# A reordered opening of a fused attention and FFN kernel: context first, K's and V's projections ahead of the queries', signs on ACT, slot 1 in another order

## What is computed

```python
q = layernorm(x) @ Wq    # 32 heads of 128
k, v = ctx @ Wk, ctx @ Wv    # 8 heads of 128, each shared by 4 query heads
q, k = rotary(q, pos), rotary(k, pos)
a = softmax(where(mask == 0, -1e9, q @ k.T / sqrt(128))) @ v
x = x + a @ Wo
h = layernorm(x)
r = softmax(h @ gate_w.T)        # 8 experts
return x + (h * (r @ in_scale)) @ sign(W).T * (r @ out_scale) + bias
```

## Time and profile before

| | |
|---|---|
| median of 3 runs | 1199.98 us (1199.96 to 1200.46) |
| the profiled execution | 1200.44 us |
| its span, first to last instruction | 1197.4 us |
| PE busy | 1162.7 us, 97% |
| DVE, POOL, ACT busy | 810.1, 712.2, 551.7 us |
| mean granted clock of PE | 0.988 of 2.4 GHz |

### The profile page before, as it was taken

One profiled execution on the slowest core, in us unless ns is written; L12 is line 12 of the kernel. 1 busy time (PEld: TensorE's weight loads), 2 busy tenths in 40 slices (PEclk: granted clock), 3 DMA queues, 4 the chain that ended last, 5 costly groups with the idle time before them and its releaser, 6 DMA issues.

```text
span 1197.4 us, 23749 instructions
## 1 busy us (share of the span) xinstructions
PE 1162.7 (97%) x7636; PEld 951.1 (79%) x7636; DVE 810.1 (68%) x1367; ACT 551.7 (46%) x1768; POOL 712.2 (59%) x593
## 2 busy tenths in 40 slices
PE   5799999999999999999999999999999999999996
PEld 4588888888888888887888888888888888888875
DVE  6767677666776666676766677667667666666663
ACT  3445445444453544444544444544454354444432
POOL 5666655555666655765555675655666565676515
PEclk8899999999999999999999999999999999999997
DMA  8234332232422223433322322323332221222200
GB/s 219 86 110 119 96 98 87 80 92 80 120 89 71 79 79 88 128 101 93 98 76 72 95 90 77 105 80 96 88 98 88 62 79 62 87 83 89 66 2 35
DMA packets 136923, 106.02 MB, mean 89 GB/s; under 512 B 12776, under 2 KB 111080, under 8 KB 136864
## 3 DMA queue, kind: packets, MB, share of 16 engines
q1 hardware_dynamic: 131488, 94.78, 27.0%
q10 hardware_dynamic: 4608, 8.39, 2.1%
q0 software_dynamic: 768, 2.10, 0.5%
HBM read 101.05 MB, written 4.19 MB: 88 GB/s over the span
## 4 chain that ended last, share of the span: by engine, by line
PE 87%; DVE 9%; POOL 2%; issue 1%; ACT 1%; DMA 1%; POOLq 0%; DVEq 0%; SPq 0%; ACTq 0%
PE chunk L1037 23%; PE chunk L1038 22%; PE chunk L1039 22%; PE o_ps L1110 4%; DVE swp L793 3%; PE sc_ps L1085 3%; PE tr_ps L1085 2%; PE aux L1026 2%; PE o_ps L1026 2%; DVE qT L795 1%; PE sc_ps L1026 1%; PE tr_ps L1026 1%; PE aux L1187 1%; PE aux L1188 1%; DVE oT_lo L728 1%
## 5 line engine op out<-in xcount | busy, mean ns | idle before, releaser
L404 POOL TENSOR_TENSOR w_lo<-raw,w_hi 128x512 fp32r<-128x512 f32 x192 | 247.2, 1299 | 385.3 <-ACT w_hi L503 385.3
L793 DVE TENSOR_TENSOR swp<-chunk,sinT 64x512 f32<-64x512 f32 x320 | 220.4, 689 | 98.7 <-PE chunk L1039 94.7
L1037 PE MATMUL chunk<-xT_hi,w_hi 128*128 128x512 f32 (+1 forms) x512 | 211.6, 413 | 2.0 <-POOL w_lo L404 1.9
L1038 PE MATMUL chunk<-xT_lo,w_hi 128*128 128x512 f32 (+1 forms) x512 | 201.9, 394 | 0.0
L1039 PE MATMUL chunk<-xT_hi,w_lo 128*128 128x512 f32 (+1 forms) x512 | 201.1, 393 | 0.0
L1037 PE MATMUL chunk<-wo_hi,oT_hi 128*128 128x512 f32 x496 | 196.6, 396 | 0.4 <-issue 0.4
L411 POOL TENSOR_TENSOR qT<-qT,swp 128x512 f32<-128x512 f32 x128 | 165.9, 1296 | 47.1 <-DVE qT L795 44.9
L1039 PE MATMUL chunk<-wo_hi,oT_lo 128*128 128x512 f32 x496 | 193.7, 390 | 0.0
L1038 PE MATMUL chunk<-wo_lo,oT_hi 128*128 128x512 f32 x496 | 193.2, 390 | 0.0
L539 ACT ACTIVATE probs<-scores,neg_max 128x64 f32<-128x64 f32 x512 | 170.4, 335 | 28.2 <-DVE neg_max L750 28.2
L735 DVE TENSOR_TENSOR acc<-chunk,acc 128x512 f32 (+1 forms) x128 | 88.2, 689 | 139.9 <-PE chunk L1039 139.5
(11 more groups left out here) (281 smaller groups left out, 1936.7 us busy)
## 6 DMA issues: line engine op xcount, KB each, us to landing
raw<-in_L_xattn_Wo SPq DMA_DIRECT2D x132, 256.0 KB, 2.6
raw<-in_L_xattn_Wq SPq DMA_DIRECT2D x128, 256.0 KB, 2.7
raw<-in_L_xattn_Wk SPq DMA_DIRECT2D x32, 256.0 KB
raw<-in_L_xattn_Wv SPq DMA_DIRECT2D x32, 256.0 KB
acc<-in_x ACTq DMA_DIRECT2D x16, 256.0 KB, 2.9
c_tile<-in_ctx SPq DMA_DIRECT2D x12, 256.0 KB, 3.1
x_tile<-in_x SPq DMA_DIRECT2D x12, 256.0 KB, 3.4
result<-y ACTq DMA_DIRECT2D x12, 256.0 KB, 2.1
```

The lines of the kernel that those rows point to most:

```text
L404: nc.gpsimd.tensor_tensor(lo, raw[:, n % RING, :], hi.bitcast(F32), ALU.subtract).then_inc(wsplit_lo, 1)
L793: last = nc.vector.tensor_tensor(swp[to, k, :], bank[of, :], sinT[to, here], ALU.mult)
L1037: nc.tensor.matmul(bank, a_hi, b_hi, start=i == 0, stop=False)
L1038: nc.tensor.matmul(bank, a_hi, b_lo, start=False, stop=False)
```

## The change

- Loads: context tiles 0 and 1 come first on SP's queue, 2 and 3 first on ACT's; then Wk, x tiles 0 and 1, Wv and the queries' weights on SP, x tiles 2 and 3 and the positions on ACT's. ffn_weight is loaded before the mask.
- Slot 0 loads six weights in the order K, V, queries (`FIRST_STREAM`), and none of wo. K is projected right behind the context's transposes; V behind x's and the rotary rows' transposes, then the queries.
- POOL computes s_rstd between the second and the third gather. The zeroing of buffers comes later, and the small FFN tables use other buffers (f_tile, fT).
- The signs are made by ACT (`ACT.Sign`), one instruction each.
- Slot 1 has lists of its own on PE, ACT and DVE (`first_attention`): K's projection before the scores, the others at other places; `scales_lo` and the copies of `ffn_constants` come later.
- The weights' ring in later slots is numbered anew (`ring_use`, `split_count`), with the same distance between a load and the split that it waits for.

```diff
-    PLACE = [STREAM.index(c) for c in range(CH)]
-    assert CH % RING == 0 and PROJ % WRING == 0 and BT == 512 and 2 * S == P and KVH == TJ + PAIRS + 2
+    FIRST_STREAM = [0, PROJ - 1, 1, 2, 3, 4]
...
-        in_raw, out_raw, gate_raw, sign_scratch = vT, probs[:, 0, :], c_tile, probs[:, 1, :]
+        in_raw, out_raw, gate_raw = f_tile, fT, c_tile
...
-        C_BANK, X_BANK = [aux, sc_ps, tr_ps, o_ps[0]], [chunk[0], chunk[2], o_ps[1], aux]
-        ROWS_BANK, SGN_BANK, GATE_BANK = [sc_ps, tr_ps], [sc_ps, tr_ps, o_ps[0], aux], o_ps[1]
+        C_BANK, X_BANK = [aux, sc_ps, tr_ps, o_ps[0]], [chunk[2], o_ps[1], sc_ps, aux]
+        ROWS_BANK, SGN_BANK, GATE_BANK = [tr_ps, o_ps[0]], [o_ps[0], sc_ps, tr_ps, aux], o_ps[1]
...
+        def loads_of(s):
+            return FIRST_STREAM if s.first_proj else STREAM if s.proj else [PROJ + h for h in range(HG)]
+        def ring_use(s, n):
+            return (n % RING, n // RING + 1) if s.first_proj else ((n - HG) % RING, 2 * s.U + (n - HG) // RING + 1)
+        def split_count(s, n):
+            return n + 1 if s.first_proj else s.U * CH - HG + n + 1
+        def rank(s, j):
+            return FIRST_STREAM.index(j) if s.first_proj else j
+        def proj_bank(s, j):
+            return chunk[0 if s.first_proj and j == PROJ - 1 else PROJ_BANK[j]]
...
-                for n in range(CH):
-                    if s.first_proj and n == RING:
-                        load_constants()
-                    c, r = STREAM[n], n % RING
+                for n, c in enumerate(loads_of(s)):
+                    r, _ = ring_use(s, n)
                     if c >= PROJ:
                         grp = (s.g + KVH - 1) % KVH if isinstance(s.g, int) else s.g - 1
                     else:
                         grp = s.g
                     if not (s.first_proj and n < RING):
-                        sp.wait_ge(wsplit_lo, s.U * CH + n - RING + 1)
+                        sp.wait_ge(wsplit_lo, split_count(s, n) - RING)
                     if c < PROJ:
                         src = (wk_c[:, :, bass.ts(grp, D)] if c == 0 else
                                wv_c[:, :, bass.ts(grp, D)] if c == PROJ - 1 else
@@ -331,6 +349,11 @@
                         sp.dma_start(raw[:, r, :].rearrange("p (c n) -> p c n", n=P), src).then_inc(raw_in[r], 16)
                     else:
                         sp.dma_start(raw[:, r, :], wo[bass.ts(grp * HG + (c - PROJ), D), :]).then_inc(raw_in[r], 16)
+                    if s.first_proj and n == 0:
+                        for p in range(2):
+                            sp.dma_start(acc[:, p, :], row_of(x_t, p)).then_inc(x_first_in[p], 16)
+                if s.first_proj:
+                    load_constants()
...
             def load_constants():
+                sp.dma_start(fw, ffn_w.rearrange("(c p) n -> p c n", p=P)).then_inc(fw_in, 16)
                 load_mask(0)
-                sp.dma_start(fw, ffn_w.rearrange("(c p) n -> p c n", p=P)).then_inc(fw_in, 16)
                 sp.wait_ge(zeros_ok, 4)
...
-            sp.dma_start(pos_i[:, :], pos.rearrange("(n b) s -> (b s) n", b=2),
-                         allow_slow_non_contiguous=True).then_inc(pos_in, 16)
-            for p in range(PAIRS):
+                        r, _ = ring_use(s, h)
+                        sp.wait_ge(wsplit_lo, split_count(s, h) - RING)
+                        sp.dma_start(raw[:, r, :], wo[bass.ts((KVH - 1) * HG + h, D), :]).then_inc(raw_in[r], 16)
+            for p in range(2):
                 sp.dma_start(c_first[:, p, :], row_of(ctx_t, p)).then_inc(c_first_in[p], 16)
...
-            wait_alone(pool, pos_first_ok, 1)
-            for p in range(PAIRS):
-                gather_rows(rows_first[:, p, :], pos_first[:, p:p + 1]).then_inc(rows_first_in, 16)
-            for zeros in (gate_raw[:, :], in_raw[:, :], out_raw, route[:, :]):
-                nc.gpsimd.memset(zeros, 0.0).then_inc(zeros_ok, 1)
-            pool.wait_ge(consts, 1)
-            pool.wait_ge(x_st3, PAIRS)
-            nc.gpsimd.tensor_tensor(s_rstd[:, :], s_var[:, :], half[:, :], ALU.pow).then_inc(x_st4, PAIRS)
...
+            def first_projections(s):
+                for n in range(3, PROJ):
+                    split_lo(s, n)
+                    rope_sum(s, n - 3)
+                rope_sum(s, KQ - 2)
+                rope_sum(s, KQ - 1)
             def slot(s):
                 t, f, residual = jobs_of(s)
+                if s.first_proj:
+                    return first_projections(s)
...
+            def first_quarter():
+                first = Slot(0, 0, False, False)
+                split_lo(first, 0)
+                wait_alone(pool, pos_first_ok, 1)
+                for p in range(PAIRS):
+                    if p == 2:
+                        pool.wait_ge(consts, 1)
+                        pool.wait_ge(x_st3, PAIRS)
+                        nc.gpsimd.tensor_tensor(s_rstd[:, :], s_var[:, :], half[:, :], ALU.pow).then_inc(x_st4, PAIRS)
+                    gather_rows(rows_first[:, p, :], pos_first[:, p:p + 1]).then_inc(rows_first_in, 16)
+                split_lo(first, 1)
+                split_lo(first, 2)
+                pool.wait_ge(x_tr, PAIRS)
+                for zeros in (gate_raw[:, :], in_raw[:, :], out_raw[:, :], route[:, :]):
+                    nc.gpsimd.memset(zeros, 0.0).then_inc(zeros_ok, 1)
+                wait_alone(pool, rows_tr, PAIRS)
+                nc.gpsimd.memset(scores[:, :, :], MASKED).then_inc(fill_ok, 1)
+            first_quarter()
...
-                act.wait_ge(proj_done, (s.U + 1) * PROJ)
-                if s.first_proj:
-                    act.wait_ge(sc_lo, 2)
-                else:
+                act.wait_ge(proj_done, s.U * PROJ + rank(s, PROJ - 1) + 1)
+                if not s.first_proj:
                     act.wait_ge(v_tr, s.U)
-                copy(vT[:, :], chunk[PROJ_BANK[PROJ - 1]][:, :]).then_inc(vT_ok, 1)
+                copy(vT[:, :], proj_bank(s, PROJ - 1)[:, :]).then_inc(vT_ok, 1)
...
+            def first_attention(s):
+                ffn_constants()
+                split_hi(s, 0)
+                split_hi(s, 1)
+                v_in_rows(s)
+                split_hi(s, 2)
+                exp_duo(s, 0)
+                exp_duo(s, 1)
+                for n in range(3, 6):
+                    split_hi(s, n)
+                pT_hi_split(s, 0)
+                split_hi(s, 6)
+                split_hi(s, 7)
+                pT_hi_split(s, 1)
+                out_hi(s, 0)
+                out_hi(s, 1)
+                split_hi(s, 8)
+                split_hi(s, 9)
+                v_out(s)
+                out_hi(s, 2)
+                out_hi(s, 3)
+            def first_projections(s):
+                split_hi(s, 3)
+                v_out(s)
+                split_hi(s, 4)
+                act.wait_ge(fw_in, 16)
+                for c in range(EC):
+                    nc.scalar.activation(fw[:, c, :], fw[:, c, :], ACT.Sign).then_inc(fw_sgn, 1)
+                split_hi(s, 5)
...
-                act.wait_ge(sc_in, 16 * 6)
-                copy(in_sc[:, :], in_raw[:, :]).then_inc(sc_hi, 1)
-                copy(out_sc[:, :], out_raw).then_inc(sc_hi, 1)
                 for c in range(EC):
                     act.wait_ge(fw_tr, c + 1)
                     copy(sgnT[:, c, :], SGN_BANK[c][:, :]).then_inc(fw_ok, 1)
+                act.wait_ge(sc_in, 16 * 6)
+                copy(in_sc[:, :], in_raw[:, :]).then_inc(sc_hi, 1)
+                copy(out_sc[:, :], out_raw[:, :]).then_inc(sc_hi, 1)
...
             def first_quarter():
                 for p in range(PAIRS):
                     act.wait_ge(c_tr, p + 1)
                     copy(cT_hi[:, :, bass.ts(p, P)], by_chunk(C_BANK[p])).then_inc(c_hi, 1)
-                split_hi(first_slot, 0)
+                    if p == 1:
+                        split_hi(first_slot, 0)
+                split_hi(first_slot, 1)
                 for p in range(PAIRS):
                     act.wait_ge(x_tr, p + 1)
                     copy(xT_hi[:, :, bass.ts(p, P)], by_chunk(X_BANK[p])).then_inc(x_hi, 1)
-                split_hi(first_slot, 1)
+                split_hi(first_slot, 2)
                 for i in range(PAIRS // 2):
                     act.wait_ge(rows_tr, 2 * i + 2)
                     scaled(cosT[:, bass.ts(i, 2 * P)], ROWS_BANK[i][:, 0:2 * P])
                     scaled(sinT[:, bass.ts(i, 2 * P)], ROWS_BANK[i][:, 2 * P:4 * P]).then_inc(rope_ok, 2)
-            for p in range(PAIRS):
+            for p in (2, 3):
+                nc.scalar.dma_start(c_first[:, p, :], row_of(ctx_t, p)).then_inc(c_first_in[p], 16)
+            for p in (2, 3):
                 nc.scalar.dma_start(acc[:, p, :], row_of(x_t, p)).then_inc(x_first_in[p], 16)
+            nc.scalar.dma_start(pos_i[:, :], pos.rearrange("(n b) s -> (b s) n", b=2),
+                                allow_slow_non_contiguous=True).then_inc(pos_in, 16)
...
+            def first_attention(s):
+                v_lo_split(s)
```

(88 more changed lines are left out.)

59 lines of the change are left out of this document (23 added, 36 removed).

## The result

Against the kernel before on the same chip (20 runs each), the changed kernel took 1201.51 us in the median and the kernel before 1199.39: a ratio of 1.0016, with a 95% interval of 1.001 to 1.0023. So it is slower by 2.1 us, where 1.3 us less was forecast. The changed kernel once more, in a later set of 11 runs, gave 1.0014 (1.0004 to 1.0023). The profiled execution has a span of 1200.2 us (before: 1197.4).

A forecast was written before the change was run, and what follows sets the result against it. TensorE (PE), busy 97%, was taken as the bound. The first output projection's start, 72.5 + 0.8 (V later) + 0.6 (clock) = 73.9 against 75.16, gave -1.3 us: 1198.7 us, 8-in-10 range 1195.4 to 1202.8.

The forecast's parts named there:

- Context, K's projection: Opening: first context tile lands at 4.3 us; K's projection starts at 11.3 and ends at 16.4, 2.86 us of work gained.
- Positions: Opening, last on ACT's queue: 2.7 us behind x tile 3, landing at 10.8; x_st3 at 13.8, against 14.8 before.
- Gathers' landing: Opening, tables 2 and 3: the last gather lands 3.9 us after issue, at 21.6; bounds 2.9 and 6.3.
- The slower rival: Opening: last gather takes 6.3 us, V's projection waits for tables until 25.7, cold clock +1.7; 1202.7 us; chance 0.11.
- Clock before V: PE idle between 19.0 and 21.7 us, ahead of V's projection: a clock fall costs 0.6 us, bounds 0 and 1.7.
- From V to T: V's projection (22.8 us) to the first output projection (73.9): slot 0, constants and slot 1, with new waits.
- T: Start of the first output projection: forecast 73.9 us against 75.16 before, so -1.3 us.
- the third query's: Slot 1: PE waits 2.5 us before the third query; a clock fall there would be absorbed almost whole (0.1 to 0.2).
- the scales' wait: Slot 1: values(1) waits for scales_lo, behind out_lo on DVE, from 68.85 to 71.5 us; 1.3 less without contention.
- Behind T nothing changes: From the first output projection on, order, instructions and relative waits stay; 1122.2 us of the span stay.
- Sign's table, the signs on ACT: ACT: four signs of 0.5 us each hidden; rival: Sign needs another table load, +1.3 us, 1200.0 us, chance 0.05.
- my forecast's case: The main case: first output projection starts between 72.8 and 77.5 us; chance 0.50.

The follow-up runs named there:

- the filled gap: The changed kernel with 14 matmuls, result unused, on PE in the gap ahead of slot 1's first projection; 1200.51 us, ratio 1.0009 to the kernel before.
- all four edits: The changed kernel with positions first, V's projection behind K's, slot 1's first weight earlier, PE's wait for scales later; 1192.05 us, ratio 0.9942 to the kernel before.

## Why the prediction was wrong, point by point

- **Context, K's projection: right.** First transpose at 4.42 (4.3), K at 11.28 (11.3), K's end at 15.9 (16.4).
- **Positions: wrong, the first failed term.** Landing counted at 10.8, seen by DVE at 14.10. I had taken a transfer of 4-byte pieces as 2.7 us behind its queue's last tile, from its time when it had hardly any work beside it. Beside the weights' queue only as many of its pieces went as of theirs of 512 bytes (1784 and 1789 in 4 us). From there everything shifts: s_var 16.53 (13.8), x normalised 19.39 (16.2), V at 25.26 (22.8). The statement that the 1.0 us won on s_var "is spent in POOL's queue" was made of the wrong sum: s_var came 1.9 us later than before, not earlier.
- **Gathers' landing: sooner than taken, at the lower bound.** Tables are transposed from 23.64 with no wait, so the last gather landed 2.8 us or less behind its issue at 20.88 (3.9 taken, bounds 2.9 and 6.3). The DMA had drained by then (66 GB/s from 20 to 22). The slower rival's V start (25.7) was nearly met at 25.26, by another cause than its own: late issue, not a late landing.
- **Clock before V: the cost was elsewhere.** I had 0.6 us for it. V itself ran at full clock, but x's and the tables' transposes, from 20.05 to 25.26, ran at half: x's take 3.6 us, where I had 2.1 (16.9 to 19.0).
- **From V to T: right, with some luck in the sum.** 25.26 to 76.25 is 50.99 us, forecast 51.1. But 0.6 of the 51.1 was the clock ahead of V, which did not come there; without it the forecast is 50.5, and two waits were 0.3 longer than taken. The wait ahead of slot 1's first projection was 3.83 (3.55), with the fall of the clock (1.6, by the filled gap 1.6); the third query's 2.82 (2.5); the fourth's 1.12 (1.1; the text says five instructions of POOL there, but its sum and the trace have four); the scales' wait 2.53, behind an out_sc of 1.74 and an in_sc of 1.07. T's error is that of V's start: 76.25 against 73.9 is 2.35, and V's start was off by 2.46; with the positions first V starts at 22.47, in time.
- **"Behind T nothing changes": wrong, the second failed term.** Order and instructions are the same, but not how PE arrives at T. The text put a fall of the clock into the wait of the third query, where it would have been absorbed, and none into the scales' wait, which it named. It fell behind the scales' wait (4.45 us for twelve matmuls of 2.78), and not behind the third query's. The waits that could absorb it lie ahead of T, so all of the 1.7 us counts.
- **Sign's table, the signs on ACT: right.** One ACT_TABLE_LOAD in the trace after, as before, and four signs of about 0.55 us (four in 2.18), behind which no wait of PE stands in slot 0. By the Trainium skill (ScalarE: Activation LUTs, Table sets) cheap functions are in every set; that no second load came agrees.
- **The case that came.** T lies within my forecast's case (72.8 to 77.5), near its end. With the two terms put right, 73.9 + 2.35 + 1.7 behind it against 75.16, the sum is +2.8 us, the spans' difference; in the medians 2.1.

The change's idea, work moved ahead of x, was worth 2.9 us. V's start, 2.6 us late, took nearly all of it (with the positions first it is back at 22.47), and the new standstills took more. With the positions first it is level with the kernel before (1.0002); with slot 1's first weight made in time it is 0.4% faster.

## What to carry to other kernels

Put a transfer of many small pieces where little runs beside it, here at the head of its queue, even if it is the smallest load: count its pieces and not only its bytes, and count what hangs behind its consumer in each queue. When work is moved forward, look at the first operand of the next stage in the same way: a gap of PE can cost more than its length. Here gaps of 3.83 and 2.53 us cost some 1.6 us more through the clock, and one of 2.82 in the same kernel nothing more, so read the granted clock behind each gap. And a stretch "where nothing changes" begins only where the waits just ahead of it are the same too.

## What the runs showed of the hardware

- Two DMA queues moved equal numbers of pieces of unequal size: 1789 and 1784 in 4 us, 0.89 and 0.01 MB; the rate is 225 GB/s there, and 379 from 4.8 to 6 us of the same trace. The same 8 KB transfer took 4.0 us first and 11.4 last.
- A first gather's issue on POOL took 1.42 us beside DVE's norms and 1.14 in the kernels before and after; later ones 0.95 to 1.04. The other way round, in the kernel with all four edits, a 128x16 TENSOR_SCALAR of DVE took 1.29 us (12.27; 0.17 in the kernel after), while POOL made a low split (12.25 to 13.53).
- Between the end of pos_first on DVE (14.90) and POOL's first gather (15.87), which waits for it, lie 0.97 us in the kernel after, where later gathers follow one another by 0.30.
